# Moving one of ScalarE's load issues behind its table load in an adapter and low-rank feed-forward kernel

## What is computed

```python
base = einsum('btd,od->bto', x, W)                       # W: 1024 x 1024
logits = einsum('btd,ed->bte', x, Wr) + 5.0 * one_hot(language_ids)
topw, topi = top_k(logits, 2);  weights = softmax(topw)
gates = sum(one_hot(topi) * weights)
h = einsum('btd,erd->bter', x, A)                        # 8 experts, rank 16
c = base + 2.0 * einsum('bter,bte,eor->bto', h, gates, B)
weight = U * S @ V.T                                     # rank 256
out = x + einsum('bti,oi->bto', c, weight)
```

## Time and profile before

| | |
|---|---|
| median of 3 runs | 153.99 us (153.8 to 154.09) |
| profiled execution, its own time | 154.44 us |
| span of its instructions | 152.7 us |
| TensorE matmuls, busy | 147.4 us (97%) |
| VectorE, GpSimd, ScalarE, busy | 107.2, 72.3, 63.5 us |
| HBM read, written | 24.16 MB, 8.39 MB |

### The profile page before, as it was taken

The page is one execution under the profiler, slowest core; times in us unless marked ns, Lnnn a source line. Parts: engine busy times, 40 slices in busy tenths (PEclk is TensorE's granted clock), DMA queues, the critical chain, the costliest instruction groups (busy, mean ns, idle before and its releaser), DMA issues.

```text
span 152.7 us, 2912 instructions
## 1 busy us (share of the span) xinstructions
PE 147.4 (97%) x1056; PEld 139.1 (91%) x1056; DVE 107.2 (70%) x297; ACT 63.5 (42%) x141; POOL 72.3 (47%) x57
## 2 busy tenths in 40 slices
PE   7799999999999999999999999999999999999991
PEld 5699999999999989998999899989999998998880
DVE  0488887759478999978765875587558736795851
ACT  4397876894546422446014612351334105013000
POOL 2000242993560659292966186636655640721700
PEclk9999999999999999999999999999999999999998
DMA  5999999999303030049719903980591068006184
GB/s 171 315 400 409 400 405 411 410 407 409 132 6 137 0 137 4 0 192 345 288 60 350 386 34 136 338 347 10 211 286 57 0 277 262 17 0 275 69 339 142
DMA packets 10670, 32.72 MB, mean 214 GB/s; under 512 B 1441, under 2 KB 1953, under 8 KB 10529
## 3 DMA queue, kind: packets, MB, share of 16 engines
q1 hardware_dynamic: 10368, 31.96, 55.8%
q10 hardware_dynamic: 288, 0.59, 1.2%
HBM read 24.16 MB, written 8.39 MB: 213 GB/s over the span
## 4 chain that ended last, share of the span: by engine, by line
PE 93%; DMA 3%; ACT 0%; DVE 0%; SPq 0%; issue 0%; DVEq 0%
PE fin L343 13%; PE fin L345 13%; PE fin L344 13%; PE pj L344 10%; PE pj L343 10%; PE pj L345 10%; PE zt L343 6%; PE zt L345 6%; PE zt L344 6%; DMA w_raw<-in_W 3%; PE gt L447 1%; PE zt L434 1%; PE fin L380 1%; PE gt L344 1%; PE gt L345 1%; PE fin L390 1%
## 5 line engine op out<-in xcount | busy, mean ns | idle before, releaser
L281 POOL TENSOR_TENSOR xT_lo<-xt_raw,xT_hi 128x1024 fp32r<-128x1024 f32 x15 | 36.5, 2443 | 25.2 <-DVE gh L801 7.9
L304 POOL TENSOR_TENSOR x_all<-x_all,vw_raw 128x512 f32<-128x512 f32 x21 | 26.6, 1297 | 25.8 <-DVE vw_raw L849 25.8
L343 PE MATMUL pj<-proj_hi,xT_hi 128*128 128x264 f32 x128 | 36.9, 288 | 0.0
L344 PE MATMUL pj<-proj_lo,xT_hi 128*128 128x264 f32 x128 | 36.3, 284 | 0.0
L345 PE MATMUL pj<-proj_hi,xT_lo 128*128 128x264 f32 x128 | 36.2, 283 | 0.0
L343 PE MATMUL fin<-v_hi,w_hi 128*128 128x256 f32 (+1 forms) x80 | 25.7, 321 | 0.0
L344 PE MATMUL fin<-v_lo,w_hi 128*128 128x256 f32 (+1 forms) x80 | 25.6, 320 | 0.0
L345 PE MATMUL fin<-v_hi,w_lo 128*128 128x256 f32 (+1 forms) x80 | 25.6, 320 | 0.0
L344 PEld LDWEIGHTS pj<-proj_lo,xT_hi 128*128 128x128 f32 x128 | 24.1, 189 | 0.2
L343 PEld LDWEIGHTS pj<-proj_hi,xT_hi 128*128 128x128 f32 x128 | 24.1, 188 | 0.2
L345 PEld LDWEIGHTS pj<-proj_hi,xT_lo 128*128 128x128 f32 x128 | 24.0, 188 | 0.0
(11 more groups left out here) (100 smaller groups left out, 282.5 us busy)
## 6 DMA issues: line engine op xcount, KB each, us to landing
xt_raw<-in_xt SPq DMA_DIRECT2D x16, 512.0 KB, 7.6
x_all<-in_x SPq DMA_DIRECT2D x16, 512.0 KB, 6.5
out<-x_all SPq DMA_DIRECT2D x13, 512.0 KB, 3.2
vw_raw<-in_VW SPq DMA_DIRECT2D x6, 384.0 KB, 7.1
w_raw<-in_W SPq DMA_DIRECT2D x8, 256.0 KB, 6.6
out<-x_all SPq DMA_DIRECT2D x5, 256.0 KB, 2.0
w_raw<-in_U SPq DMA_DIRECT2D x1, 1024.0 KB, 8.8
aw_raw<-in_AW SPq DMA_DIRECT2D x1, 544.0 KB, 7.2
```

The source lines that it names most:

```text
L281: nc.gpsimd.tensor_sub(xT_lo[:, t % XTR, :, :], xt_raw[:, t % XTR, :, :], xT_hi[:, t % XTR, :, :].bitcast(F32)).then_inc(xt_lo, 1)
L304: nc.gpsimd.tensor_add(x_all[:, t % XR, cols], x_all[:, t % XR, cols], ups[:, j, :]).then_inc(side_add, 1)
L343: nc.tensor.matmul(dst, l_hi, r_hi, start=first, stop=False, skip_group_check=shared)
L344: nc.tensor.matmul(dst, l_hi, r_lo, start=False, stop=False, skip_group_check=shared)
```

## The change

The issue of `vw_raw` k = 1 moves from in front of the one-column exponential to behind the wait for its end.

```diff
             first = RANK + P
             act.dma_start(vw_raw[:, 0, first:], VW[0, :, first:]).then_inc(vw_rest_load, 16)
-            act.dma_start(vw_raw[:, 1, :], VW[1, :, :]).then_inc(vw_load[1], 16)
             act.wait_ge(const, 3 + E)
             nc.scalar.activation(esum[:, :], iota_e[:, 0:1], ACT.Exp).then_inc(act_warm, 1)
             act.wait_ge(act_warm, 1)
+            act.dma_start(vw_raw[:, 1, :], VW[1, :, :]).then_inc(vw_load[1], 16)
             for i in range(2 * OC):
```

## The result

The changed kernel takes **155.96 us** in the median of six executions (155.41 to 157.59), the kernel before 154.01 beside it (153.35 to 154.46): slower by the ratio 1.0153, with a 95% interval of 1.0097 to 1.0209, and 1.95 us between the medians. I had forecast 153.85 in a range of 153.3 to 154.9. The profiled execution took 157.17 us, its span is 155.4.

The account below looks back on a forecast made before the run. TensorE was taken as the bound, with only its waits at the start movable. Piece 2 starting at 8.44 instead of 8.60 gave -0.16 us, carried over to the median of 153.99: 153.85 us, range 153.3 to 154.9.

Parts of the forecast that it names:

- What bounds the kernel: TensorE, busy 147.4 of 152.7 us; a change at the start only moves when it never waits again.
- the meeting point of two loads: Piece 2 starts at the later of piece 1's end and 1.14 us after `vw_raw` k = 1 lands.
- `w_raw` k = 0 freed: Before piece 1: this load lands by 4.9 to 5.3, not 6.13; the 0.87 us gap closes wholly or nearly.
- what `vw_raw` k = 1 loses: Before piece 2: issued at 2.70, the load starts moving at 4.7 and lands at 7.3, bounded by 5.7 and 9.2.
- L: Landing time of `vw_raw` k = 1: 7.46 in the profile before, forecast 7.3; piece 2 is ready 1.14 us later.
- my own sum: Whole kernel: -0.16 us from piece 2 starting at 8.44 instead of 8.60; beyond L = 7.46 loss is one for one.
- a ring of its own: Second queue: its load waits for its turn in a separate ring, taken to speak against the upper bound of 9.2.
- the base: The change was reckoned from the profiled execution, 154.44 us, and carried over to the runs' median, 153.99, 0.45 us lower.
- The second, the load late behind SyncE's: Before piece 2: `vw_raw` k = 1 lands after 7.77, TensorE waits there; 154.3 to 155.7 us, chance 0.32.
- L = 9.4: Before piece 2: landing of `vw_raw` k = 1 if the 2.4 us tail of its transfer recurs after 7.0.
- The first (0.30): Before piece 2: `vw_raw` k = 1 catches up and lands before 7.15; 153.1 to 153.7 us, chance 0.30.
- The third, a drain behind the table load: ScalarE: a further 1.28 us pause delays the issue to 4.0, landing at 8.6; 155.1 us, chance 0.02.

Follow-up runs that it names:

- e12: The kernel before, profiled once more with no edit: 153.23 us.
- e8: The changed kernel, profiled once more with no edit: 155.54 us.
- e5: The changed kernel with the issue of `vw_raw` k = 1 in front of the wait for the exponential's end: 155.85 us, ratio 1.0113 to the kernel before.
- e11: The changed kernel with two loads swapped, SyncE issuing `vw_raw` k = 1 at 1.65, ScalarE `w_raw` k = 1 at 2.70: 155.06 us, ratio 1.0074 to the kernel before.
- e2: The changed kernel with eight matmuls of zeros on zeros between pieces 1 and 2: median 155.76 us, ratio 1.0134 to the kernel before.

## Why the prediction was wrong

*What bounds the kernel* was right: no wait behind the first pieces in either kernel, and what piece 2 loses reaches the end (2.25 us of it, 2.31 us of time, in e12 and e8). Also right: piece 2 as the meeting point of two loads, the 1.14 us from landing to start (9.90 - 8.82 = 1.08 after), the table load moved for nothing, the issue at 2.70, and `w_raw` k = 0 freed.

*The step that failed* is "what `vw_raw` k = 1 loses": L = 7.3 was 8.82 in the profile, 8.7 in e8. The transfer was to begin 2 us after the issue, at 4.7, and began after 3, at about 5.8; the rest of the difference is its late end. By my own sum L = 8.82 is 155.3, over the range. I argued from the load issued at 1.16, when hardly anything stood in the first queue. The rows of SyncE's loads issued at 2.11 and 2.58, 6.4 and 6.5 us, were issued under nearly the same load, and 6.0 to 6.1 us was close to them. I discarded them because the second queue has a ring of its own. e5 and e11 show that it gave no precedence: 6.8 and 6.3 us from issue to landing.

*The second failure was the base.* I noticed that the runs were 0.35 to 0.64 us shorter than the profiled execution and made of it only a lesser gain. It could have warned me that L = 7.46 need not recur. With L = 5.6 as in e12, piece 2 has some 0.8 us in hand, and L = 7.3 gives 8.44 against 7.50: 0.9 us slower in such an execution, not 0.16 faster. Against the median the step is smaller. By the pair e12 and e8 the time follows piece 2, so the median of 154.01 stands for a piece 2 at about 8.3 (an estimate: 7.50 + 154.01 - 153.23), and my own L = 7.3 for some 154.2 us. So the base turned the sign, from slightly slower to slightly faster; it did not take the time out of the range of 153.3 to 154.9.

*The third part was missing*: the clock. I wrote that TensorE's waits alone count and gave the idle stretch no price beyond its length. It cost about 1.5 us more in the profiled execution, and a second of the six has the same mean clock; without these two the median would be 155.77 and not 155.96. That the idle stretch is what lowers the clock is supported by e2 and not proven.

*The rivals.* The second, the load late behind SyncE's, with a chance of 0.32, is what happened; its price with L = 8.8 was 155.3, and the base and the clock can make up the difference. The measured time lies over this rival's own range, 154.3 to 155.7. I had mentioned L = 9.4 there, which by my sum is 155.9 and should have been the upper end; that it comes close to the median of 155.96 is luck, since the load landed at 8.8. The first (0.30) and the forecast (0.36) fall. The third, a drain behind the table load, fell: the exponential ran at 2.46 and the issue followed at 2.70.

## What to carry to other kernels

In these runs a load's time to land went by what stood ahead of it on either queue when it was issued and by what was issued close behind it. So price a moved issue by the loads issued near its new time, on whichever queue, and not by its own time at its old place. Where the profiled execution differs from the runs' median by more than the effect that is to be predicted, ask which of its waits would recur, and take a second profile; a second one can be as far off on the other side, as e12 is. An idle stretch of TensorE can be followed by a lower clock and so come with a cost beyond its length.

## What was not expected of the hardware

- Between an issue at 1.16 us and one at 1.92 lies a step: the same 384 KB landed at 5.6 (7.46 in the trace of before) and at 8.7. How the DMA engines share turns such that a load on the second queue, with one load ahead, is spread over more than 4 us (e5) is left open; only the company was varied, not the engines' order.
- With the second queue silent in 4 to 5 us, the first moved no more for it: 237 GB/s in the changed kernel, where both together moved 336 in the trace of before and 376 in e12.
- The matmuls at the start reached their full pace at different times in executions of the same program (piece 0's last four took 0.64 us in the first profile of the changed kernel and 0.84 in e8), while the granted clock reads full in both. An early full pace makes the gap in front of piece 2 longer, and the two profiles with the long gap (2.4 and 2.3 us, e5) have a fall of the clock behind it; the one with 1.42 has none. What decides it is left open.
